# Expert loops written out, products of constants between gate and attention, mixing over 128 rows

## The reference

```python
x = x + gate(group_norm(x))           # channel and spatial gate
x = attention(x)                      # 8 heads of 16, all 256 points of an image, + residual
t = t + window_attention(ln(t))       # causal, window of 64
t = t + experts2(ln(t))               # 16 experts, 2 per token, see below
t = t + causal_linear_attention(ln(t))
t = t + experts3(ln(t))               # 8 experts, 1 per token: gelu(x W1 + b1) W2 + b2, times max prob

# experts2: per expert the mean of silu(x w1^T) over its tokens, times w2^T;
# a token gets the softmax-weighted sum of the two experts' mean outputs
h_mean = einsum('tef,te->ef', silu(einsum('td,efd->tef', x, w1)), mask) / counts
out = einsum('tk,tkd->td', routing_w, einsum('ef,edf->ed', h_mean, w2)[top_idx])
```

## Time and profile before

| | us |
|---|---|
| median of 3 runs | 904.35 |
| lowest and highest | 902.98, 909.2 |
| span of the profiled execution | 927.6 |
| TensorE busy in it | 743.2 (80%) |
| VectorE, ScalarE, GpSimd busy | 605.4, 419.7, 428.7 |

### The profile page before, as it was taken

The page is one execution under the profiler, slowest core; times in us unless marked ns, Lnnn a source line. Parts: engine busy times, 40 slices in busy tenths (PEclk is TensorE's granted clock), DMA queues, the critical chain, the costliest instruction groups (busy, mean ns, idle before and its releaser), DMA issues. The chain is left out here.

```text
span 927.6 us, 22686 instructions
## 1 busy us (share of the span) xinstructions
PE 743.2 (80%) x7923; PEld 581.3 (63%) x7924; DVE 605.4 (65%) x1590; ACT 419.7 (45%) x865; POOL 428.7 (46%) x561
## 2 busy tenths in 40 slices
PE   1567899999999999999755677677699888439994
PEld 1244666666667777777544566675477666329993
DVE  3763467777766666766488476676656776727764
ACT  0452355555554444444263344451376666124442
POOL 0336002222227766777604666640455687714551
PEclk9975699999999999999675799996699999659997
DMA  5920000000000000000001111140700000112216
GB/s 163 274 89 0 1 2 1 2 2 1 2 2 2 8 14 13 14 13 19 23 1 26 42 45 43 42 31 1 208 1 2 7 19 19 45 54 71 63 51 182
DMA packets 38417, 37.16 MB, mean 40 GB/s; under 512 B 4915, under 2 KB 30632, under 8 KB 38324
## 3 DMA queue, kind: packets, MB, share of 16 engines
q1 hardware_dynamic: 31348, 24.35, 9.0%
q0 software_dynamic: 4864, 9.47, 4.5%
q10 hardware_dynamic: 2112, 2.10, 0.7%
HBM read 26.89 MB, written 9.52 MB: 39 GB/s over the span
## 5 line engine op out<-in xcount | busy, mean ns | idle before, releaser
L821 DVE TENSOR_REDUCE attend_negmax<-ps 128x4 f32<-128x1024 f32 (+1 forms) x128 | 139.8, 1092 | 100.3 <-PE ps L561 99.8
L744 ACT ACTIVATE attend_prob<-ps 128x1024 f32<-128x1024 f32 (+1 forms) x128 | 110.6, 864 | 163.9 <-PE ps L578 163.6
L561 PE MATMUL ps<-attend_key,attend_query 32*128 32x256 f32 (+2 forms) x1024 | 132.4, 377 | 11.2 <-DVE attend_negmax L821 10.0
L578 PE MATMUL ps<-attend_query,attend_key 32*128 32x256 f32 (+2 forms) x1024 | 129.7, 349 | 0.0
L561 PEld LDWEIGHTS ps<-attend_key,attend_query 32*128 32x128 f32 x1024 | 83.5, 193 | 54.3 <-issue 49.5
L1810 POOL DMA_INDIRECT sums_xs<-table,sums_source x80 | 82.0, 1025 | 72.1 <-DVE sums_source L1744 33.2
L1529 PE MATMUL ps<-sums_xT,sums_own 128*128 128x128 f32 x640 | 88.1, 288 | 33.0 <-ACT sums_hidden L1871 23.0
L1529 PEld LDWEIGHTS ps<-sums_xT,sums_own 128*128 128x128 f32 x640 | 82.1, 201 | 38.5 <-DVE sums_own L1518 29.5
L570 PE MATMUL ps<-attend_maxT,pick 32*128 32x256 f32 (+2 forms) x512 | 101.6, 393 | 0.5 <-ACT attend_prob L744 0.5
L578 PEld LDWEIGHTS ps<-attend_query,attend_key 32*128 32x128 f32 x1024 | 79.2, 189 | 0.3
L498 POOL TENSOR_SCALAR attend_rstd<-attend_spread 128x2 f32<-128x2 f32 x32 | 7.3, 230 | 151.7 <-DVE attend_spread L871 151.7
(11 more groups left out here) (355 smaller groups left out, 1767.7 us busy)
## 6 DMA issues: line engine op xcount, KB each, us to landing
w<-in_L_ffn_w SPq DMA_DIRECT2D x1, 4096.0 KB, 27.9
expert_xs<-slots SPq DMA_DIRECT2D x40, 64.5 KB
x<-in_x ACTq DMA_DIRECT2D x4, 512.0 KB, 8.5
table<-rows SPq DMA_DIRECT2D x16, 128.0 KB
experts<-in_L_ffn_W SPq DMA_DIRECT2D x1, 2048.0 KB, 8.5
experts<-in_L_ffn_W SPq DMA_DIRECT2D x4, 512.0 KB, 9.5
rows<-outputs SPq DMA_DIRECT2D x8, 256.0 KB, 4.9
out<-expert_result SPq DMA_DIRECT2D x8, 256.0 KB, 2.8
```

The source lines that it names most:

```text
L561: return nc.tensor.matmul(ps[:, SCORE + i, at:at + width], query[rows, n % 3, a * 128:(a + 1) * 128], key[rows, n % 3, odd, from_:from_ + ...
L578: return nc.tensor.matmul(ps[:, KEY_SCORE + i, at:at + width], key[rows, n % 3, odd, b * 128:(b + 1) * 128], query[rows, n % 3, from_:from ...
L744: nc.scalar.activation(of_pair(t // 4, t % 4)[:, :, 0:wide], ps[:, KEY_SCORE:KEY_SCORE + 2, 0:wide], ACT.Exp).then_inc(prob_ready, 1)
L821: last = nc.vector.tensor_reduce(out=negmax[:, s // 4 % 2, :, r:r + 2, odd].rearrange("p a r -> p r a"), in_=ps[:, SCORE:SCORE + 2, 0:2 * ...
```

## The change

- Both numbers of slots are no longer rounded up to a multiple of 8: S2 becomes 79, S3 becomes 39. The ordering still works with an even number, 80.
- `slot_loop` is replaced by `each_slot`, which writes all slots out for every engine; every threshold is a constant.
- `keep_clock` issues products of 128 x 128 by 128 x 512 of a constant in bf16 into a bank that is not in use: four ahead of each of the last two `turn_out` and six behind them in the gate stage, five behind `project(0)` and five in each of the steps 0 to 4 of attention, between the scoring and the rest of the step.
- `partial` has 128 slots in place of 80; GpSimd zeroes those from 79 on, and the transposes, the copies and the mixing products of `mix_means` have 128 rows.

```diff
 def slot_tiles(experts, taken):
-    most = (TOKENS * taken + experts * 127) // 128
-    return most + -most % 8
+    return (TOKENS * taken + experts * 127) // 128

+S2_EVEN = S2 + S2 % 2

+def keep_clock(nc, bank, eye, products):
+    for _ in range(products):
+        nc.tensor.matmul(bank, eye[:, 0:128], eye[:, 0:512], start=True, stop=True)

@@ spatial_gate, TensorE
                 for m in (IMAGES // 2 - 2, IMAGES // 2 - 1):
+                    keep_clock(nc, ps[:, 7, :], window, 4)
                     turn_out(m)
+                keep_clock(nc, ps[:, 7, :], window, 6)

@@ attend, TensorE
                 project(0)
+                keep_clock(nc, ps[:, KEY_SCORE, :], window_mask, 5)
                 for s in range(4 * (COUNT + 7)):
                     n, j = s // 4, s % 4
                     if s < SLOTS + LAG:
                         score_pairs(s)
+                    if s < LAG:
+                        keep_clock(nc, ps[:, KEY_SCORE, :], window_mask, 5)

 def past(s, tiles):
-    return not isinstance(s, int) or s >= tiles
-
-def slot_loop(engine, count, step):
-    for r in range(BODY):
-        step(r, r)
-    with engine.Fori(1, count // BODY - 1) as i:
-        for r in range(BODY):
-            step(BODY * i + r, r)
-    for r in range(BODY):
-        step(count - BODY + r, r)
+    return s >= tiles
+
+def each_slot(count, step):
+    for s in range(count):
+        step(s, s % BODY)

@@ expert_sums (expert_outputs likewise: slot_loop(engine, ...) -> each_slot(...))
-        source = sb("source", [128, S2], UINT32)
+        source = sb("source", [128, S2_EVEN], UINT32)
                 cast_constants(pool)
+                nc.gpsimd.memset(partial[:, S2:128, :], 0.0).then_inc(rest_cleared, 1)
...
-                slot_loop(dve, S2, step)
-                total(S2 - 1, BODY - 1)
+                    if s == 0:
+                        dve.wait_ge(rest_cleared, 1)
+                each_slot(S2, step)
+                total(S2 - 1, (S2 - 1) % BODY)

@@ mix_means (and every other [S2, ...] or [0:S2] of it likewise)
-        choice = sb("choice", [S2, E2], FP32R)
+        choice = sb("choice", [128, E2], FP32R)
-                    mm = nc.tensor.transpose(ps[0:S2, 1, c * 128:(c + 1) * 128], partial[:, :, c], consts["ident"][:])
+                    mm = nc.tensor.transpose(ps[:, 1, c * 128:(c + 1) * 128], partial[:, :, c], consts["ident"][:])
-                    own = choice[:, e:e + 1].to_broadcast([S2, 128])
+                    own = choice[:, e:e + 1].to_broadcast([128, 128])

@@ build
-        partial = sb("partial", [128, S2, FC])
+        partial = sb("partial", [128, 128, FC])
```

More of the change, by code:

```diff
@@ L85, in link_on, with spatial_gate @@
     return link
-def spatial_gate(nc, x, stats, x_measured, load_experts, w, xf, tokens, consts, ps):
+def spatial_gate(nc, x, stats, x_measured, load_experts, w, xf, tokens, consts, window, ps):
     with stage(nc, "gate") as (sb, sem):
@@ L1793, in expert_sums @@
         (cast_constants, number_tiles, count, invert, exponential, choose, order, weigh_choices,
-         source_ready) = ordering(nc, sb, sem, E2, K2, S2, logits, None, consts, tile_expert, source, ps, spare, weight,
+         source_ready) = ordering(nc, sb, sem, E2, K2, S2_EVEN, logits, None, consts, tile_expert, source, ps, spare, weight,
                                   inverse, tile_choice, choice=choice)
@@ L1798, in inside @@
         def inside(s):
-            return not isinstance(s, int) or s < S2
+            return s < S2
         with nc.Block() as block:
@@ L1845, in step @@
                     multiply_up(nc, pe, own, 4, xT, own_ready, xT_ready, hidden_ready, up_done, ps, UP, s, r)
-                slot_loop(pe, S2, step)
+                each_slot(S2, step)
             @block.scalar
@@ L1871, in step @@
                     nc.scalar.activation(hidden[:, r % 2, :], ps[:, UP + r % 2, :], ACT.Silu).then_inc(hidden_ready, 1)
-                slot_loop(act, S2, step)
+                each_slot(S2, step)
             @block.vector
@@ L1967, in _ @@
                 act.wait_ge(partial_turned, 1)
-                nc.scalar.activation(partial_high[:], ps[0:S2, 1, :], ACT.Copy).then_inc(high_ready, 1)
+                nc.scalar.activation(partial_high[:], ps[:, 1, :], ACT.Copy).then_inc(high_ready, 1)
             @block.vector
@@ L1973, in _ @@
                 dve.wait_ge(partial_turned, 1)
-                nc.vector.tensor_copy(choice[:], tile_choice[0:S2, :]).then_inc(low_ready, 1)
+                nc.vector.tensor_copy(choice[:], tile_choice[:]).then_inc(low_ready, 1)
                 dve.wait_ge(high_ready, 1)
-                nc.vector.tensor_tensor(partial_low[:], ps[0:S2, 1, :], partial_high[:].bitcast(FP32),
+                nc.vector.tensor_tensor(partial_low[:], ps[:, 1, :], partial_high[:].bitcast(FP32),
                                         ALU.subtract).then_inc(low_ready, 1)
@@ L2031, in inside @@
         def inside(s):
-            return not isinstance(s, int) or s < S3
+            return s < S3
         with nc.Block() as block:
@@ L2053, in load @@
                     sp.dma_start(xs[:, r, :], slots[bass.ds(at, 128), :]).then_inc(loaded[r], 16)
-                slot_loop(sp, S3, load)
+                each_slot(S3, load)
                 for r in range(BODY):
-                    sp.wait_ge(stored[r], 16 * S3 // BODY)
+                    sp.wait_ge(stored[r], 16 * len(range(r, S3, BODY)))
                 for g in range(8):
@@ L2102, in step @@
                         down(s - 2, (r - 2) % BODY)
-                slot_loop(pe, S3, step)
-                down(S3 - 2, BODY - 2)
-                down(S3 - 1, BODY - 1)
+                each_slot(S3, step)
+                down(S3 - 2, (S3 - 2) % BODY)
+                down(S3 - 1, (S3 - 1) % BODY)
                 for g in range(8):
@@ L2132, in step @@
                     nc.scalar.activation(hidden[:, r % 4, :], before[:, r % 2, :], ACT.Gelu).then_inc(hidden_ready, 1)
-                slot_loop(act, S3, step)
+                each_slot(S3, step)
                 for g in range(8):
@@ L2178, in step @@
                         finish(s - 2, (r - 2) % BODY)
-                slot_loop(dve, S3, step)
-                finish(S3 - 2, BODY - 2)
-                finish(S3 - 1, BODY - 1)
+                each_slot(S3, step)
+                finish(S3 - 2, (S3 - 2) % BODY)
+                finish(S3 - 1, (S3 - 1) % BODY)
                 for g in range(8):
@@ L2376, in load_second @@
             sp.dma_start(w2[:], a["L2_ffn_w2"].rearrange("e d f -> d e f")).then_inc(experts_in, 16)
-        spatial_gate(nc, x, x_stats, x_measured, load_second, w, xf, tokens, consts, ps)
+        spatial_gate(nc, x, x_stats, x_measured, load_second, w, xf, tokens, consts, window, ps)
         first_input.close()
```

6 lines of the change are left out of this document (3 added, 3 removed).

## The result

The changed kernel takes 894.0 us (median of four runs, 891.1 to 895.0) against 904.6 for the kernel before beside it (four runs, 903.0 to 909.2). The medians differ by 10.6 us. The ratio on record is 0.9864 with a 95% interval of 0.9839 to 0.9889, which is 12.3 us less (10.0 to 14.6); so the gain is 11 to 12 us.

What follows compares the result with a forecast made beforehand. It took TensorE as bound in attention and the last expert stage, with a half-clock attention head and a stalling first expert stage between. Terms -8.5 - 1.9 - 1.5 - 0.5 = -12.4 us took 904.35 to 892, range 873 to 903.

Steps and rivals of the forecast that it cites:

- Products, -8.5 us: Gate stage and attention head: 44 products of constants keep TensorE at full clock, 8.5 us less, bounds 5 to 9.3.
- One slot less in the last stage, -1.9: Last expert stage: 39 slots instead of 40 save one slot of TensorE, which never idles there, 1.89 us.
- One slot less in the first, -1.5: First expert stage: 79 slots instead of 80 save one gather, issued 1.5 us apart.
- The loop, 0: First expert stage: writing out the loop gains nothing, as gathers in flight cause the stalls; bound -17 us otherwise.
- written-out slots 4 and 5: First expert stage: already written-out slots stalled worst, ScalarE waiting 4.03 us, which spoke against the loop as cause.
- The sign that I had named: First expert stage: the forecast is wrong if the 1.5 us between gathers falls towards 1.24.
- rival (a): First expert stage: the loop causes TensorE's late reports, so writing it out gives 17 us more, 875 us; chance 0.17.
- Code fetch, 0: Written-out code: fetching it costs 0, judged by attention's straight code, 9 fetches in 97 us with TensorE 97% busy.
- Mixing, -0.5: Mixing over 128 rows: full clock may return and speed the transpose and first spreading products, 0.5 us less, bounds 0 to 1.5.
- (b): Attention head: clock stays at half despite the products, +11 us, 912 us; chance 0.14 together with a change bringing only its slots.
- (c): Written-out expert slots: code is fetched too slowly while the same transfer engines gather, 924 us; chance 0.04.
- (d): Attention head: the clock comes back, but late, and the gain is 5 us less, 897; chance 0.62 together with the forecast.

Runs made afterwards that it cites:

- both with 56 slots: Kernel before with only 56 of the first expert stage's 80 slots run, once looped, once all written out: 873.4 us looped, 870.8 written out.
- two in place of five: Changed kernel with two products of constants instead of five at each of six places in attention, the gate's 14 kept: 893.9 us, ratio 0.9878.
- more products: Changed kernel with 62 more products of constants, behind the mixing, around the linear attention and ahead of the last expert stage: 893.4 us, ratio 0.9872.

## Why the prediction was right, and where not

1. **Products, -8.5 us.** Right as mechanism, and the working held to the step: seven steps 18.9 us as forecast, full clock from the gate on. The eighth maximum came at 99.2 instead of "near 98", because the part ahead of the steps gained 1.4 us and not 2.1: the gate's last six products held `project(0)` up from 76.38 to 76.84, the 0.46 us that I had bounded by 0.5 and taken as 0. The first gather moved 497.2 to 488.5, 8.7 us. But this is the gain against one execution. In seven traces without working products (the two of before, both with 56 slots, the loop written out, the mixing alone, the changed kernel without products) the first gather starts between 492.1 and 497.5, mean 494.2, and the trace of before was a late one; in the four with them (changed, products only, two in place of five, more products) it is 487.0 to 488.5, mean 487.4. That is 6.8 us on average, and up to 2 us of the forecast were luck of the profile. The reason stands in the same traces: the clock came back by itself at 98.6 to 102.0 us in five of the seven, in which the seven steps took 22.8 to 23.1 us, and only in the first profile and in the one with the loop written out at 107.5 and 107.8, with 26.1. The kernel before, profiled again:

```profile
75.97:99.86 23.89, 19.28 (x78) 12.51 (x78) 8.59 (x14) 3.65 (x7) 11.18 (x9) 0.50 0.00 0
99.90:107.50 7.60, 5.54 (x67) 3.96 (x65) 4.46 (x7) 4.00 (x5) 0.00 (x0) 1.00 0.01 2
```

By time it is 8.5 (5.7 to 11.3), which does not tell 6.8 from 8.5.
2. **One slot less in the last stage, -1.9.** A slot measured 1.90, and the stage is 2.0 us shorter where the clock comes back equally late.
3. **One slot less in the first, -1.5.** The term was mis-sized: it is 1.28. I divided 119.8 us of a disturbed stage by its slots. Its bound was in the text, 0.94 + 0.30 = 1.24.
4. **The loop, 0.** Nearly right: -0.5 to -0.9. The argument from the written-out slots 4 and 5 pointed the right way. What failed is the forecast for the changed profile, that the stalls of 1.9 us and the 1.5 us between gathers would still be there. The sign that I had named for rival (a) appeared without its cause, and only the second profile of the kernel before shows that. The step at fault is the treatment of span against median: I wrote down 927.6 beside 904.35 and carried the difference of 23 us along as a constant. It was no constant: 18.0 us of it lay in the one stage whose rows I was interpreting. Profiled again, the span is 903.0 us and the time of that same run 904.8.
5. **Code fetch, 0.** Right. The whole changed kernel makes 66 and 40 instruction transfers where the kernel before makes 59 and 34, and between 500 and 590 us TensorE has no wait for "issue" in its written-out slots. The Trainium skill, "Runtime: NRT & Kernel Launch", section on instruction fetch mechanics, recommends writing loops out because of the fetch at a taken branch; here, by the distances of the gathers, it is worth some 0.01 us a slot.
6. **Mixing, -0.5.** Wrong by its size, at the edge of its bounds: 0 by time (from 1.2 us less to 4.2 more), and by the traces perhaps 0.3 more. The clock came back as supposed, and was gone again before the instructions that should gain. I had asked whether it returns, not what TensorE does between its return and the place of use. "TensorE: Matmul & The Clock Gate" of the Trainium skill, section "What's actually happening", has activity release the clock; here products of 128 rows did, while TensorE stayed at half over 10.4 us of products of 80 rows with no pause, and over 36.6 us of mostly 32 rows, 90% busy.

The sum with the measured terms, -6.8 - 1.9 - 1.3 - 0.7 - 0, is -10.7 us. The medians say -10.6, the ratio -12.3 (-10.0 to -14.6). So my -12.4 is no better supported than -10.7: where it agrees with the ratio, it does so through terms that were too large (products by 1.7, mixing by 0.5, first-stage slot by 0.2) against one that was too small (the loop by 0.7).

Of the rivals, (b) is the one with substance: its +11 became +5 by time when the products had 32 rows, with 24.0 us in place of 26 for the five steps. (c) and (d) did not occur in the changed kernel. Two figures of the working don't hold: seven steps in 26.07 us are 3.72 each, not 3.71; and 0.19 us over 118 slots is 22 us, while undoing 12.4 takes 0.105 (0.19 fits the 64 looped slots). The 1.3 us for a fetch stall in (c) is in no row.

## What to carry to other kernels

Products of constants paid here where a chain of two engines started cold, TensorE had waits to put them in, and what followed at once used the clock; products of 128 rows did it where those of 32, and 10.4 us of pauseless work of 80, did not; and where TensorE waited again before the work that should gain, they brought nothing. Writing out a loop whose pace was set by another engine brought under 1 us. If the span of a profile stands 2% above the median, profile again before a row of it becomes a term of a sum.

## What the runs showed of the hardware

- Columns and busy share being equal, the rows of a product made the difference for the clock: 44 products of 128 x 512 kept it at 2.4 GHz, the same of 32 x 512 left it at 1.2 GHz for 36.6 us with TensorE 90% busy. Rows of zeros seem to count too: mixing over 80 rows left it at half for 30.7 to 37.6 us in nine traces, over 128 rows, in four traces, it did so for 6.8 us or not at all before the products were done.
- The same program had its clock back at 99.9 us in one execution and at 107.5 in another, its code and data being the same. The scatter of its times goes with this: over 66 runs of the kernel before (901.4 to 911.3 us) the time falls as the mean granted clock of the run rises, with a correlation of -0.88; the 17 runs at 0.911 or more have a median of 902.4 us, the 14 at 0.901 or less one of 909.7.
- One execution of the kernel before took 1.52 us a gather where all others took 1.28 to 1.29, ScalarE waiting 1.9 us for TensorE after every third slot. Its cause is open.
